# A cross-attention kernel: the third score tile of six slots is issued behind the half denominator product

## The reference

```python
x = (hidden_states - mu) * rsqrt(var + 1e-05) * ln_gamma + ln_beta
Q = split_heads(x @ Wq.T)            # 32 batches, 32 heads, 56 queries, 16
K = split_heads(memory_keys)         # 32 batches, 32 heads, 1500 keys, 16
V = split_heads(memory_values)
scores = einsum('bhsd,bhtd->bhst', Q, K) * 16 ** -0.5
scores = where(mask, scores, -inf)
probs = softmax(scores, axis=-1)
out = (einsum('bhst,bhtd->bhsd', probs, V) -> B,S,HIDDEN) @ Wout.T
return hidden_states + out
```

## Time and profile before

| | |
|---|---|
| runs, median (lowest to highest) | 1474.55 us (1472.51 to 1477.33) |
| the profiled execution: own time, span | 1475.04 us, 1473.3 us |
| granted TensorE clock over the span | 0.992 of full |
| PE busy | 1391.1 us, 94% |
| weight loads busy | 992.9 us, 67% |
| DVE busy | 1072.2 us, 73% |
| ACT busy | 751.6 us, 51% |
| POOL busy | 1242.8 us, 84% |
| DMA, mean | 153 GB/s |

### The profile page before, as it was taken

The page is one execution under the profiler, slowest core; times in us unless marked ns, Lnnn a source line. Parts: engine busy times, 40 slices in busy tenths (PEclk is TensorE's granted clock), DMA queues, the critical chain, the costliest instruction groups (busy, mean ns, idle before and its releaser), DMA issues.

```text
span 1473.3 us, 66063 instructions
## 1 busy us (share of the span) xinstructions
PE 1391.1 (94%) x30000; PEld 992.9 (67%) x30000; DVE 1072.2 (73%) x3356; ACT 751.6 (51%) x623; POOL 1242.8 (84%) x434
## 2 busy tenths in 40 slices
PE   6999999999999999999999999999999999999986
PEld 4337677676766767676676767676676767677675
DVE  6657777777777777777777777777777777777730
ACT  2125555555555555545555555554555555555553
POOL 1009998989999898989989898998989899898986
PEclk9999999999999999999999999999999999999999
DMA  9303444435444443444444444444344443444320
GB/s 296 80 38 141 176 165 146 171 135 183 158 166 166 148 171 141 174 161 156 176 164 152 155 156 166 172 151 166 149 160 158 162 171 148 175 159 152 147 86 8
DMA packets 39161, 224.90 MB, mean 153 GB/s; under 512 B 4546, under 2 KB 4578, under 8 KB 26882
## 3 DMA queue, kind: packets, MB, share of 16 engines
q1 hardware_dynamic: 38882, 220.68, 41.3%
HBM read 216.90 MB, written 3.77 MB: 150 GB/s over the span
## 4 chain that ended last, share of the span: by engine, by line
PE 68%; DVE 24%; ACT 4%; issue 3%; POOL 1%; DMA 0%; ACTq 0%; SPq 0%; POOLq 0%; DVEq 0%
PE ps L234 20%; DVE masked L335 18%; PE ps L289 17%; PE ps L274 12%; PE ps L303 6%; PE ps L251 5%; PE ps L266 4%; PE ps L664 4%; ACT probs L370 3%; DVE den_inv L359 3%; PE ps L242 1%; POOL sums L422 1%; DVE tile_max L335 1%; DVE stats L555 0%; DVE probs L572 0%
## 5 line engine op out<-in xcount | busy, mean ns | idle before, releaser
L335 DVE CUSTOM_DVE_ANT_0 masked<-ps,mask_tile 112x500 bf16<-112x500 f32 x1536 | 974.9, 672 | 310.1 <-PE ps L234 295.5
L370 ACT ACTIVATE probs<-ps,mask_bias 125x1792 f32<-125x1792 f32 x384 | 674.2, 1756 | 629.3 <-PE ps L274 607.1
L422 POOL TENSOR_TENSOR sums<-sums,probs 125x1792 f32<-125x1792 f32 x191 | 763.5, 3997 | 10.1
L422 POOL TENSOR_TENSOR sums<-probs 125x1792 f32<-125x1792 f32 x96 | 383.7, 3997 | 197.3 <-ACT probs L370 197.3
L234 PE MATMUL ps<-kT,qdb 32*112 32x500 bf16 x1536 | 487.7, 414 | 43.8 <-DVE tile_max L335 41.4
L274 PEld LDWEIGHTS ps<-qd,kT 32*125 32x125 f32 x12288 | 433.9, 185 | 1.6 <-issue 0.3
L274 PE MATMUL ps<-qd,kT 32*125 32x112 f32 x12288 | 432.7, 269 | 2.4 <-issue 2.4
L289 PE MATMUL ps<-probs,v 125*32 125x112 f32 x12288 | 372.9, 262 | 1.2 <-ACT probs L370 0.7
L289 PEld LDWEIGHTS ps<-probs,v 125*32 125x32 f32 x12288 | 299.2, 110 | 68.7 <-issue 44.8
L234 PEld LDWEIGHTS ps<-kT,qdb 32*112 32x112 bf16 x1536 | 157.9, 123 | 245.6 <-DVE tile_max L335 184.0
L266 PE MATMUL ps<-max_rows,ones_row 4*125 4x448 bf16 x1536 | 189.6, 389 | 12.7 <-ACT probs L370 9.8
(11 more groups left out here) (49 smaller groups left out, 254.6 us busy)
## 6 DMA issues: line engine op xcount, KB each, us to landing
kT<-in_kt SPq DMA_DIRECT2D x96, 1000.0 KB, 5.2
v<-in_ctx SPq DMA_DIRECT2D x96, 1000.0 KB
mask_tile<-mask_add SPq DMA_DIRECT2D x32, 328.1 KB, 13.6
x_res<-in_x SPq DMA_DIRECT2D x16, 224.0 KB, 14.1
out<-result SPq DMA_DIRECT2D x16, 224.0 KB, 14.1
probs<-in_x SPq DMA_DIRECT2D x14, 224.0 KB, 9.2
v<-in_wq_t SPq DMA_DIRECT2D x1, 1024.0 KB, 5.9
woutT<-in_wout_t SPq DMA_DIRECT2D x1, 1024.0 KB, 20.7
```

The source lines that it names most:

```text
L335: nc.vector.tensor_tensor_reduce(out=masked[0:PAIR_Q, t % 2, :], in0=bank[0:PAIR_Q, 0:KEYS], in1=mask_tile[0:PAIR_Q, b % 2, KEYS * c:KEYS ...
L370: nc.scalar.activation(probs[0:LANES, k % PROBS], ps[0:LANES, 0:TILES_R, 0:BANK_Q], ACT.Exp, bias=mask_bias[0:LANES, n:n + 1], scale=SCALE ...
L422: nc.gpsimd.tensor_tensor(total, before, probs[0:LANES, slot % PROBS], ALU.add).then_inc(summed, 1)
```

## The change

In the six slots that hold half a denominator product, the third score tile is no longer issued right behind the second but behind the half product. In all other slots the order stays.

```diff
                     score_blocks(pe, b, k, range(BLOCKS))
+                    half_product = k >= 6 and (k - 6) % GROUP < 2 or k in (2, 3) and b > 0
                     if tiles:
                         score_tile(pe, tiles[1])
-                        score_tile(pe, tiles[2])
+                        if not half_product:
+                            score_tile(pe, tiles[2])
                     if k == ROWS_SLOT + 1 and b < end:
 
                         pe.wait_ge(rows_taken, b + 2)
                     if k >= 6 and (k - 6) % GROUP < 2:
                         add_denominators(pe, b, (k - 6) // GROUP, (k - 6) % GROUP)
                     elif k in (2, 3) and b > 0:
                         add_denominators(pe, b - 1, SUMS - 1, k - 2)
+                    if tiles and half_product:
+                        score_tile(pe, tiles[2])
                     if k == ROWS_SLOT and b < end:
                         turn_rows(pe, b + 1)
```

## The result

| | before | changed | ratio, 95% interval |
|---|---|---|---|
| first comparison, 9 runs each | 1472.87 us | 1479.35 us | 1.0033 [1.0019, 1.0047] |
| second, on another occasion, 25 and 12 runs | 1474.73 us | 1477.33 us | 1.0024 [1.0014, 1.0035] |
| profiled span | 1473.3 us | 1473.7 us | |

The changed kernel is slower by 0.2 to 0.3%, 3.5 to 5 us by the ratios (the medians differ by 6.5 and 2.6 us). The forecast was 1479.0. But the two profiled spans are the same to 0.4 us, at mean granted clocks of 0.992 before and 0.994 changed, so the middle of the trace has to tell what the slots did, and the rest has to be found elsewhere.

A forecast was written before the change was run, and what follows sets the result against it. No engine alone was taken as the bound, but two loops: exact scores with exponential, and score tiles. Fourteen even batches by 0.26, fifteen odd by 0, batch 30 about +0.1: +3.8, say +4.0, on 1475.0 gives 1479.0 us; range 1471 to 1486.

The forecast's parts named there:

- the walk: Slot-by-slot sum of changes: +0.26 us per even batch, about 0 per odd one, +3.8, say +4.0 us in all.
- The bounds of the slots: Slot length set by exact scores and exponential (3.24 us in slot 2), or by score tiles when the first comes late.
- a late t0: First score tile less than 0.22 us ahead of the exact scores: the exponential starts 1.65 us after that tile.
- Slot 4 of odd batches: VectorE's inversions, just hidden before, would show because slot 3's last score tile comes later: +0.30 us.
- D to a tile: TensorE hand-over from half denominator product to third score tile, start to start: 0.52 us taken, between 0.41 and 0.63.
- Tile to D: TensorE hand-over from second score tile to half denominator product, start to start: 0.35 us.
- t1 to t3: Second to fourth score tile in a changed slot: 2.12 us, 2.52 in slot 10; before, 1.64 plus the VectorE wait.
- list of covers: Waits the earlier half product might expose: GpSimd's sums in slots 2, 6 and 10, with 1.26 us to spare in slot 6.
- Overlap: Faster rival: third tile loads and starts as its rows come free, hand-over 0.41 us; 1467 us, chance 0.13.
- The third tile never got in the way: Slower rival that it would: hand-over of 0.63 us or its VectorE take late; 1499 us, or 1486; chance 0.12.
- The wait was covered everywhere: Rival that the third tile still waits for VectorE: no chance worth a number, but in odd slot 10 (wait 0.6 us).
- Even and odd batches nearly equal: Sign to look for in the profile after: batch lengths of both kinds nearly the same.

The follow-up runs named there:

- the experiment on V: Changed kernel with the fourth score tile issued in the middle of the value product in the 182 half slots: 1529.68 us against 1474.34 before, ratio 1.0374.
- the order of before and the copies: Kernel before, with only four tiny 128x1 copies added ahead of ScalarE's loop: 1474.62 us against 1474.85, ratio 0.9997.
- the kernel with slots 7, 11 and odd 10: Kernel before, third tile moved behind the half product only in slots 7, 11 and odd batches' slot 10: 1468.50 us (0.9955), again 1467.76 us (0.9960).

## Why the prediction was right, and what in it was not

The sign and the size came out, 1479.0 against 1477.3 and 1479.35, but by luck in good part: the walk by itself should have given about 0, the slots that something disturbs made up for it, and the 1475.0 that the forecast started from was 2 us above the first median of before, 1472.87.

- *The bounds of the slots* were right. Each slot that was to move did, in the right direction, by within 0.04 of the walk. The rule for a late t0 (exponential at t0+1.65) held at 706.71 to 708.36. Slot 4 of odd batches, where inversions lost their cover, came out at the +0.30 that was forecast.
- *D to a tile* was the unknown cost: 0.52 taken, 0.52 found, and the experiment on V gave the same. The rule of the Trainium skill (TensorEngine Tiling (Array Packing), Key Properties) that a change of tiling mode drains TensorE agrees with that trace.
- *Tile to D* is the term of the walk that was mis-sized. I took 0.35 from tiles that had waited for VectorE, 0.42 long. t1, issued right behind the scores, is 0.38 long in slot 2 and D follows by 0.30 or 0.31; in slot 3 by 0.34. t1 to t3 was 2.08 in slot 2 and 2.11 in slots 3 and 7, not 2.12. With the 0.01 to 0.04 less, several slots just cross to where t0 does no harm: the even batch is +0.11, not +0.26, the odd one -0.14, not 0. The walk's +4 us would have been about 0 (14 x 0.11 - 15 x 0.14 = -0.6).
- *The slots that something disturbs* were not in the walk. I read one clean batch of each kind. The late exponential and the stop in slot 7 were in the trace of before, and cost almost nothing there because t0 had set the pace and left slack behind them. I walked the slack away and did not price what leaned on it: +0.19 in seven batches against a clean one, and in batches 5 and 15 what slots 8 and 10 no longer give back, +0.3 and +0.5; the rest of the +1.7 there is a longer stop, which the order of before had too in another profile. The prediction's list of covers held GpSimd's sum, but no disturbance.
- *The rivals.* Overlap is ruled out (the rows with t3 in the middle of V). The third tile never got in the way: t0 follows t3 within a row x2 of 0.42 in the half slots. The wait was covered everywhere.
- *Even and odd batches nearly equal*: 42.39 and 42.42.

Open: what sets the length of the stop of slot 7, and whether the order of the tiles does. It is 4.69 and 4.42 in batches 5 and 15 of the changed kernel against 4.25 and 3.88 before, but 4.77 and 4.31 with the order of before and the copies; two profiles of the kernel with slots 7, 11 and odd 10 have 3.79 and 3.47 for batch 15, and batch 21 has 5.02 and 5.05 changed against 5.27 before. Open with it is whether the change brings more stretches at the lower clock.

## What to carry to other kernels

Moving an instruction off a wait pays only where the wait is longer than the hand-overs that the new place adds: here about 0.5 us a slot, so two of six slots, and a third in every other batch, gained and the rest lost or gave nothing. Take such a move slot by slot. And before slack is used up, look through the whole trace, not one clean period, for what has been hidden in it.

## What the runs showed of the hardware that was not expected

- A tile on 32 rows between two products on 125 rows costs 0.48 us beyond running the products together: product to tile 0.52 from the first start of a group of four 125x224 or eight 125x112 matmuls, tile to product 0.30 to 0.35. A change between bf16 and fp32 on the same 32 rows costs nothing that the rows show (within 0.01). Two tiles in a row last 0.42 to 0.43 together, where one lasts 0.42.
- The same distance, tile to product, was 0.30 to 0.31 behind a tile of 0.38, 0.34 behind one of 0.41 and 0.35 behind one of 0.42: the product starts 0.07 or 0.08 before the end that the profile has for the tile. The 0.38 is t1 behind scores that were on time; t2 behind D has 0.42, with or without a wait for VectorE.
- Four instructions of 128 elements each, put ahead of ScalarE's loop, removed a 0.28 us delay that came back every fourth batch, some 128 ScalarE instructions apart; with slots 7, 11 and odd 10 that was worth 0.2 us a time, with the order of before nothing.
- TensorE stopped at the same place of the program in every profile (slot 7 of batches 5 and 21), with two matmuls up to 1.89 us apart, and went on 1.2 to 1.6 us behind the end of a 16 KB packet of instructions. All six stretches at the lower clock level in the middle of the profiles came with such a stop; none was seen elsewhere there.
